# Scores from two fp32r parts in two 64-row array tiles, in place of three bf16 parts in the full array

## The chip, the cores and the metric

One NeuronCore of a Trainium2 chip runs the whole program; the other cores are idle. The metric is the device time of one launch in microseconds, all loads and stores included, as the median of several runs.

## The reference, cut to what matters

The program is one transformer layer with adaptive layer norm over 16 batches of 256 tokens, 256 features, 16 heads of 16 features. Attention is causal; the feed-forward part is two experts, one with gelu and one with relu, of which each token takes one. All arrays are float32.

```python
h = layernorm(x) * (1 + ca) + sa
q = h @ w_dq.T @ w_uq.T                      # 192 wide in between
k, v = split(h @ w_dkv.T @ w_ukv.T)          # 64 wide in between
attn = softmax(einsum('bhqd,bhkd->bhqk', q, k) * 0.25 + causal_mask)
x = x + ga * (einsum('bhqk,bhkd->bhqd', attn, v) @ w_out.T)
h = layernorm(x) * (1 + cb) + sb
x = x + gb * where(top_expert == 0, ffn_gelu(h), ffn_relu(h))
```

## The kernel before

Each batch is two tiles of 128 tokens. To keep float32's precision on a matrix engine that multiplies shorter numbers, an operand is split in a high part and a rest. The projections and the experts use two fp32r parts and three products each (`product`, L333 to L335). The scores use three bf16 parts of q and of k: `SPLITS` lists the six pairs of parts that are kept, and since a head has only 16 features, the six pairs are laid under one another in the partitions: 6 x 16 = 96 rows (`R`). So one matmul over 96 rows is the sum of the six products.

The layout is made by DMA. ACT writes part 0 from PSUM (`first_part`, L743), DVE the rest and part 1 (`part_rest` L984, `second_part` L990), POOL part 2 (`q_third` L1222, `k_third` L1228). Then SyncE's queue copies each part, [128, 512] bf16, to each 16-row band of `qs` or `ks` where it is wanted (`stack`, L282): 12 transfers of 128 KB a batch. `qs` and `ks` have two buffers, by parity of the batch; `stack` of batch n waits until all score chunks of batch n-2 that read the buffer are done (`wait(sp, st_done, CH * (b.n - 1))`).

Scores are computed twice for each batch, in six chunks of 1024 PSUM columns each time:
- `s_chunk` (L382) makes rows of queries in `ps_s`. ACT copies a chunk to SBUF (L794), POOL hides what lies past the diagonal (L1246), DVE takes the row maxima (`row_max`, L933).
- `split_maxima` (L941 to L948) splits the negated maxima in three bf16 parts, `turn_maxima` (L470) transposes them on PE, ACT copies them to `mx_rows` (L774), and a DMA (`load_maxima`, L271) puts them as three more rows under `qs`, against three rows of ones under `ks`.
- `st_chunk` (L401, and the mask as a matmul L405) makes the transposed scores less the maxima in `ps_t`, now over `RM` = 99 rows; ACT takes the exponentials (L806) into `p0` and `p1`. `values` (L419, L420) multiplies them with v, four heads at a time in four 32-column tiles of the array.

Everything runs as a software pipeline over batches. Each engine has its own `step`, a list of calls written out by hand, in which `at(k)` is the batch k steps behind. Per step PE runs: `turn_maxima(at(2))`, `turn_values(at(3))`, `up`, `expand_v`, `gate`, `turn_attn`, then `st_chunk(at(2), 0)`, then `up`, `project_out(at(3))`, and from `s_chunk(at(1), 0)` on the other score chunks, mixed with the down projections, to `st_chunk(at(2), 5)`, `values(at(2), 0)`, `s_chunk(at(1), 5)`, `values`, `expand_k(at(0))`, `up(at(3), 0)`, `up(at(3), 1)`. SyncE's step issues, in this order and all to one queue: `stack_q(at(1), 2)`, `stack_q(at(0), 0)`, `stack_q(at(0), 1)`, `stack_k(at(0), 0)`, `load_gates`, `prefetch_x`, `load_maxima(at(1))`, `stack_k(at(0), 1)`, `store`, `stack_k(at(0), 2)`. `load_maxima(at(1))` in it is for the maxima that PE turns in the next step.

Of the kernel before, what the change touches and what calls it, by code (L numbers as in the profile page):

```python
# [29 lines left out]
SPLITS = ((0, 0), (0, 1), (0, 2), (1, 0), (1, 1), (2, 0))  # L30
# [23 lines left out]
def block_kernel(nc, x, w_dq, w_uqT, w_dkvT, w_ukT, w_uvT, w_outT, wgT, waT, wbT, ba, bb, cT, wmod, out):  # L54
# [13 lines left out]
    RM = R + 3  # L68
# [3 lines left out]
    LOADS = 16 * NSPLIT  # L72
# [12 lines left out]
    with ctx:  # L85
# [27 lines left out]
        parts_q, parts_k = sb("parts_q", [P, 3, KT * S], BF16), sb("parts_k", [P, 3, KT * S], BF16)  # L113
        rest_q, rest_k = sb("rest_q", [P, KT * S]), sb("rest_k", [P, KT * S])
        ckv = sb("ckv", [P, S], F32R)
        v = [sb(f"v{i}", [P, TT, NH, HD + 1]) for i in range(2)]
        qs = [sb(f"qs{i}", [RM, NH, S], BF16) for i in range(2)]
        ks = [sb(f"ks{i}", [RM, NH, S], BF16) for i in range(2)]

        score_rows = [sb(f"score_rows{i}", [P, 1024]) for i in range(2)]  # L120
        mx = sb("mx", [P, TT, NH])
        mx_parts = sb("mx_parts", [P, TT, 3, NH], BF16)
        mx_rest = sb("mx_rest", [P, TT, NH])
        mx_rows = sb("mx_rows", [3 * NH, S], BF16)
# [36 lines left out]
        cT_raw, c_silu = mx[:], mx_rest[:]  # L161
# [14 lines left out]
        q_done, q1_ready, qr_ready, q2_ready, q3_ready, k_done, k1_ready, kr_ready, k2_ready, k3_ready = (sem(n) for n in  # L176
            "q_done q1_ready qr_ready q2_ready q3_ready k_done k1_ready kr_ready k2_ready k3_ready".split())
# [52 lines left out]
        def _(sp):  # L230
# [35 lines left out]
            def load_maxima(b):  # L266

                if b.off:
                    return
                sp.wait_ge(mt_ready, b.n + 1)  # L270
                sp.dma_start(qs[b.parity][R:RM, :, :], mx_rows[:]).then_inc(maxrows_in, 16)  # L271

            def stack(b, part, side, parts, stacks, ready, done):

                if b.off:
                    return
                wait(sp, st_done, CH * (b.n - 1))
                wait_alone(sp)
                sp.wait_ge(ready[part], b.n + 1)
                for n in range(NSPLIT):  # L280
                    if SPLITS[n][side] == part:
                        sp.dma_start(stacks[b.parity][n * HD:(n + 1) * HD, :, :], parts[:, part, :]).then_inc(done[b.parity], 16)  # L282

            def stack_q(b, part):
                stack(b, part, 0, parts_q, qs, (q1_ready, q2_ready, q3_ready), q_in)

            def stack_k(b, part):
                stack(b, part, 1, parts_k, ks, (k1_ready, k2_ready, k3_ready), k_in)
# [24 lines left out]
            def step(at):  # L313
                stack_q(at(1), 2)
# [8 lines left out]
                stack_k(at(0), 2)  # L323
# [6 lines left out]
        def _(pe):  # L330
            def product(outp, left, right, start, stop, **kw):
# [7 lines left out]
                "T1": ((h32_ready, 1, 1),), "Q": ((q1_ready, 1, 1), (qr_ready, 1, 1)), "CKV": ((ckv_ready, 1, 1),),  # L339
                "K": ((k1_ready, 1, 1), (kr_ready, 1, 1)), "V": ((v_ready, 1, 1),), "MT": ((mt_ready, 1, 1),),  # L340
# [25 lines left out]
            def s_chunk(b, c):  # L366
# [12 lines left out]
                tile, heads = (0, range(8 * c, 8 * c + 8)) if c < 2 else (1, range(4 * c - 8, 4 * c - 4))  # L379
                width = P * (tile + 1)  # L380
                for n, h in enumerate(heads):
                    mm = pe.matmul(ps_s[:, n * width:(n + 1) * width], qs[b.parity][0:R, h, tile * P:(tile + 1) * P],  # L382
                                   ks[b.parity][0:R, h, 0:width], start=True, stop=True)
                mm.then_inc(s_done, 1)

            def st_chunk(b, c):
# [6 lines left out]
                if c == 0:  # L393
                    pe.wait_ge(maxrows_in, 16 * (b.n + 1))
# [5 lines left out]
                for h in range(n):  # L400
                    pe.matmul(ps_t[:, h * width:(h + 1) * width], ks[b.parity][0:RM, h0 + h, tile * P:(tile + 1) * P],  # L401
                              qs[b.parity][0:RM, h0 + h, tile * P:S], start=h % a_bank == 0, stop=False)
# [59 lines left out]
            def turn_maxima(b, *users):  # L462
# [3 lines left out]
                pe.wait_ge(max_split, 4 * (b.n + 1))  # L466
                bank_left(users)
                wait_alone(pe)
                for t in range(TT):
                    mm = pe.transpose(mt_out[:, t * P:(t + 1) * P], mx_parts[:, t, :, :].rearrange("p c h -> p (c h)"), ident_b[:])  # L470
# [185 lines left out]
            mt_out = BANK["MT"][0:3 * NH, 0:P].bitcast(BF16)  # L656
# [3 lines left out]
        def _(act):  # L660
            act.wait_ge(mod_in, 32)
            act.activation(c_silu, cT_raw, ACT.Silu).then_inc(silu_ready, 1)
# [82 lines left out]
            def q_first(b):  # L745
                first_part(b, BANK["Q"], parts_q, q_done, qr_ready, q_in, q1_ready)

            def k_first(b):
                first_part(b, BANK["K"], parts_k, k_done, kr_ready, k_in, k1_ready)
# [18 lines left out]
            def maxima_rows(b):  # L768
# [4 lines left out]
                wait(act, maxrows_in, 16 * b.n)  # L773
                act.activation(mx_rows[:], BANK["MT"][0:3 * NH, 0:P].bitcast(BF16), ACT.Copy).then_inc(mt_ready, 1)  # L774
# [21 lines left out]
            def exponentials(b, c):  # L796
# [9 lines left out]
                act.activation((p0, p1)[tile][:, h0:h0 + n, :], ps_t[:].rearrange("p (h s) -> p h s", h=n), ACT.Exp, scale=SCALE).then_inc(exp_done, 1)  # L806
# [33 lines left out]
        def _(dve):  # L840
# [81 lines left out]
            def row_max(b, c):  # L922
# [3 lines left out]
                if c == 0:  # L926

                    wait(dve, max_split, 4 * b.n)
                if c < 2:
                    dst, n = mx[:, 0, 8 * c:8 * c + 8], 8  # L930
                else:
                    dst, n = mx[:, 1, 4 * c - 8:4 * c - 4], 4
                dve.tensor_reduce(dst, score_rows[c % 2][:].rearrange("p (h k) -> p h k", h=n), AX_X, ALU.max).then_inc(max_done, 1)  # L933

            def split_maxima(b):
# [5 lines left out]
                dve.tensor_scalar(mx_parts[:, :, 0, :], mx[:], -1.0, None, ALU.mult).then_inc(max_split, 1)  # L941
                dve.wait_ge(max_split, 4 * b.n + 1)
# [371 lines left out]
```

## Time and profile before

| | |
|---|---|
| median of 3 runs | 604.27 us (600.83 to 604.54) |
| the profiled execution | 601.1 us, its span 599.3 us |
| PE busy | 520.9 us, 87% of the span, 4912 matmuls |
| PE weight loads | 446.5 us |
| DVE busy | 480.9 us, 80% |
| ACT busy | 365.5 us, 61% |
| POOL busy | 309.7 us, 52% |
| DMA queue q1 | 43760 packets, 43.19 MB, 37.2% of the 16 engines' span |
| chain that ended last | PE 31%, DVE 29%, DMA 14%, issue 11%, POOL 6% |

Busy time of PE counts each matmul with the time its result needs to come out, so a busy PE is not one at its peak; how densely matmuls follow one another is read from their start times. The pipeline fills in the first 118 us, runs evenly from there to 507 us, and drains after. A line such as `306.02 0.38 PE L405 MATMUL ... x2` in the timeline is a run of two matmuls that starts at 306.02 us and lasts 0.38 us to the end of the last.

### The profile page before, as it was taken

How to read it: one execution, taken by the hardware profiler on the slowest of the kernel's cores; microseconds unless marked ns; L12 is line 12 of the kernel's file. 1: busy time of each engine (PE TensorE's matmuls, PEld its weight loads, DVE VectorE, ACT ScalarE, POOL GpSimd, SP SyncE). 2: the span in 40 equal slices, each digit the busy share in tenths (PEclk: the TensorE clock that was granted, in tenths of full speed). 3: DMA queues.
4: the chain of work that ended last, by engine and by line, in shares of the span. 5: the costliest groups of instructions: out<-in, count | busy, mean ns of one | idle time of the engine just before them, and what ended most of it. 6: DMA issues, size and time to landing. Idle time of an engine off the chain costs nothing.

```text
span 599.3 us, 14257 instructions
## 1 busy us (share of the span) xinstructions
PE 520.9 (87%) x4912; PEld 446.5 (75%) x4912; DVE 480.9 (80%) x949; ACT 365.5 (61%) x521; POOL 309.7 (52%) x300
## 2 busy tenths in 40 slices
PE   5435757999898989999999999999999999999874
PEld 4324545788787878787878888788979788888774
DVE  3548255779798989899898999899999899887572
ACT  2424644868575866667676858585766667675320
POOL 6334223455554665655656555556665655552441
PEclk9856696999999999999999999999999999999997
DMA  8835252433516080715244251708080715210100
GB/s 246 208 39 83 25 91 55 78 67 59 104 34 128 2 161 1 128 32 93 66 67 92 48 111 28 131 5 154 0 161 2 136 26 91 53 39 2 36 19 18
DMA packets 43802, 43.74 MB, mean 73 GB/s; under 512 B 5344, under 2 KB 40800, under 8 KB 43760
## 3 DMA queue, kind: packets, MB, share of 16 engines
q1 hardware_dynamic: 43760, 43.19, 37.2%
q8 instruction: 25, 0.41, 0.3%
q14 instruction: 17, 0.14, 0.1%
HBM read 13.39 MB, written 4.23 MB: 29 GB/s over the span
## 4 chain that ended last, share of the span: by engine, by line
PE 31%; DVE 29%; DMA 14%; issue 11%; POOL 6%; ACT 4%; SPq 3%; DVEq 1%; POOLq 0%; ACTq 0%
DVE mx L933 8%; DMA xs<-x 7%; DMA qs<-mx_rows 4%; PE ps_s L382 4%; PE ps_t L401 3%; DVE z L872 3%; SPq L282 2%; DMA qs<-parts_q 2%; POOL xs L1186 2%; PE ps_c L333 2%; PE ps_t L405 2%; DVE hid L1079 2%; PE ps_o L333 2%; ACT score_rows L794 2%; PE ps_c L335 2%
## 5 line engine op out<-in xcount | busy, mean ns | idle before, releaser
L794 ACT ACTIVATE score_rows<-ps_s 128x1024 f32<-128x1024 f32 x96 | 98.9, 1031 | 78.2 <-PE ps_s L382 59.8
L1246 POOL TENSOR_SCALAR_AFFINE_SELECT score_rows<-score_rows 128x512 f32<-128x512 f32 (+1 forms) x96 | 83.0, 865 | 101.8 <-ACT score_rows L794 101.8
L933 DVE TENSOR_REDUCE mx<-score_rows 128x4 f32<-128x1024 f32 (+1 forms) x96 | 114.0, 1210 | 4.4 <-POOL score_rows L1246 4.3
L806 ACT ACTIVATE p<-ps_t 128x1024 f32<-128x1024 f32 x96 | 98.4, 1025 | 16.9 <-PE ps_t L405 16.7
L382 PE MATMUL ps_s<-ks,qs 96*128 96x256 bf16 (+1 forms) x512 | 62.6, 259 | 19.6 <-DMA qs<-parts_q 15.9
L401 PE MATMUL ps_t<-qs,ks 99*128 99x256 bf16 (+1 forms) x512 | 60.7, 253 | 15.2 <-DMA qs<-mx_rows 14.3
L1186 POOL TENSOR_TENSOR xs<-z,xs 128x512 f32<-128x512 f32 (+1 forms) x16 | 30.7, 1922 | 61.7 <-DVE z L1022 61.7
L382 PEld LDWEIGHTS ps_s<-ks,qs 96*128 96x128 bf16 x512 | 36.8, 103 | 32.0 <-DMA qs<-parts_q 17.2
L401 PEld LDWEIGHTS ps_t<-qs,ks 99*128 99x128 bf16 x512 | 38.0, 100 | 23.1 <-DMA qs<-mx_rows 10.3
L856 DVE BATCH_NORM_STATS2 ln_st<-xs 128x6 f32<-128x256 f32 (+1 forms) x64 | 23.9, 415 | 35.2 <-DMA xs<-x 27.7
L1234 POOL TENSOR_TENSOR hid_lo<-hid,hid_hi 128x512 fp32r<-128x512 f32 x32 | 42.8, 1351 | 4.8 <-DVE hid_hi L1092 4.8
L405 PE MATMUL ps_t<-past_b,ident_b 128*128 128x256 bf16 (+1 forms) x192 | 45.2, 317 | 0.0
L1177 POOL TENSOR_TENSOR ln_rs<-ln_ve,neg_half 128x2 f32<-128x2 f32 x32 | 24.2, 755 | 35.9 <-DVE ln_ve L862 35.8
L333 PE MATMUL ps_o<-wb,hid_hi 128*128 128x256 f32 x128 | 39.5, 308 | 2.3 <-DVE hid_lo L1098 2.3
L419 PE MATMUL ps_o<-p,v 128*17 128x256 f32 x512 | 41.3, 384 | 0.2 <-ACT oT L688 0.2
L1092 DVE CAST hid_hi<-hid 128x512 fp32r<-128x512 f32 x64 | 36.1, 564 | 5.0 <-ACT hid L784 4.9
L333 PE MATMUL ps_a<-wb,hid_hi 128*128 128x256 f32 x128 | 39.8, 311 | 0.0
L333 PE MATMUL ps_c<-g_hi,wa 128*128 128x256 f32 x128 | 37.6, 294 | 1.6 <-issue 1.6
L334 PE MATMUL ps_o<-wb,hid_hi 128*128 128x256 f32 x128 | 36.7, 287 | 0.0
L335 PE MATMUL ps_o<-wb,hid_lo 128*128 128x256 f32 x128 | 36.6, 286 | 0.0
L334 PE MATMUL ps_c<-g_lo,wa 128*128 128x256 f32 x128 | 36.1, 282 | 0.0
L335 PE MATMUL ps_c<-g_hi,wa 128*128 128x256 f32 x128 | 36.1, 282 | 0.0
(166 smaller groups left out, 1648.1 us busy)
## 6 DMA issues: line engine op xcount, KB each, us to landing
qs<-parts_q SPq DMA_DIRECT2D x96, 128.0 KB, 3.9
ks<-parts_k SPq DMA_DIRECT2D x96, 128.0 KB, 4.4
xs<-x SPq DMA_DIRECT2D x16, 256.0 KB, 5.3
gates<-gates_scratch SPq DMA_DIRECT2D x16, 256.0 KB, 4.6
out<-xs SPq DMA_DIRECT2D x16, 256.0 KB, 3.5
p<-wmod SPq DMA_DIRECT2D x1, 1024.0 KB, 6.3
p<-waT SPq DMA_DIRECT2D x1, 1024.0 KB, 8.7
p<-wmod SPq DMA_DIRECT2D x1, 512.0 KB, 5.2
```

The source lines that it names most:

```text
L333: pe.matmul(outp, left[0], right[0], start=start, stop=False, **kw)
L334: pe.matmul(outp, left[0], right[1], start=False, stop=False, **kw)
L335: return pe.matmul(outp, left[1], right[0], start=False, stop=stop, **kw)
L382: mm = pe.matmul(ps_s[:, n * width:(n + 1) * width], qs[b.parity][0:R, h, tile * P:(tile + 1) * P], ks[b.parity][0:R, h, 0:width], start=T ...
L401: pe.matmul(ps_t[:, h * width:(h + 1) * width], ks[b.parity][0:RM, h0 + h, tile * P:(tile + 1) * P], qs[b.parity][0:RM, h0 + h, tile * P:S ...
L405: mm = pe.matmul(diag, ident_b[:], past_b[:].unsqueeze(1).to_broadcast([P, a_bank, P]), start=False, stop=True)
L794: act.activation(score_rows[c % 2][:], ps_s[:], ACT.Copy).then_inc(scores_out, 1)
L806: act.activation((p0, p1)[tile][:, h0:h0 + n, :], ps_t[:].rearrange("p (h s) -> p h s", h=n), ACT.Exp, scale=SCALE).then_inc(exp_done, 1)
L933: dve.tensor_reduce(dst, score_rows[c % 2][:].rearrange("p (h k) -> p h k", h=n), AX_X, ALU.max).then_inc(max_done, 1)
L1186: pool.tensor_tensor(rows, gated[:], rows, ALU.add).then_inc(x1_ready, 1)
L1234: pool.tensor_tensor(hid_lo[:, 2 * u:2 * u + 2, :], hid32[:, u, :, :], hid_hi[:, 2 * u:2 * u + 2, :].bitcast(F32), ALU.subtract).then_inc( ...
L1246: pool.affine_select(out=diag, in_=diag, compare_op=ALU.is_ge, fill=NEG, base=0, pattern=[[0, n], [-1, P]], channel_multiplier=1).then_inc ...
```

## The change

- q and k are split in two fp32r parts. `SPLITS` keeps three pairs, so a head needs 48 rows. The stack buffers are fp32r and have two halves of partitions: heads of even number in the pair from row 0, the others from row `ODD` = 64, eight columns blocks (`H2`) deep.
- Each `stack` call now copies a part to each band in two transfers, one for each half. A transfer is again 128 KB. Part 0 of q goes to two bands, part 1 to one; the same for k.
- `s_chunk` and `st_chunk` issue pairs of matmuls, rows 0 to 47 (49) and rows 64 to 111 (113), each writing a PSUM bank of its own. Column counts stay 128 and 256.
- The maxima are split in two fp32r parts by two DVE instructions in place of four, transposed as f32, and loaded by two transfers.
- DVE's `part_rest` and `second_part` become one instruction (`low_part`); POOL's `q_third` and `k_third` go. SyncE's calls for the third parts go too.
- The exponentials are written to `p0` and `p1` in the order of the pairs; `ks` is filled with ones as a whole at the start.

```diff
-SPLITS = ((0, 0), (0, 1), (0, 2), (1, 0), (1, 1), (2, 0))
+SPLITS = ((0, 0), (0, 1), (1, 0))
+ODD = 64
...
-    RM = R + 3
+    RM = R + 2
+    H2 = NH // 2
...
-        qs = [sb(f"qs{i}", [RM, NH, S], BF16) for i in range(2)]
+        qs = [sb(f"qs{i}", [ODD + RM, H2, S], F32R) for i in range(2)]
...
-                sp.dma_start(qs[b.parity][R:RM, :, :], mx_rows[:]).then_inc(maxrows_in, 16)
+                for k in range(2):
+                    sp.dma_start(qs[b.parity][ODD * k + R:ODD * k + RM, :, :].bitcast(F32), mx_rows[NH * k:NH * (k + 1), :].bitcast(F32)).then_inc(maxrows_in, 16)
...
                 for n in range(NSPLIT):
                     if SPLITS[n][side] == part:
-                        sp.dma_start(stacks[b.parity][n * HD:(n + 1) * HD, :, :], parts[:, part, :]).then_inc(done[b.parity], 16)
+                        for k in range(KT):
+                            row = ODD * k + n * HD
+                            sp.dma_start(stacks[b.parity][row:row + HD, :, :].bitcast(F32), parts[:, part, k * S:(k + 1) * S].bitcast(F32)).then_inc(done[b.parity], 16)
...
             def step(at):
-                stack_q(at(1), 2)
                 stack_q(at(0), 0)
                 stack_q(at(0), 1)
                 stack_k(at(0), 0)
...
                 stack_k(at(0), 1)
                 store(at(4))
-                stack_k(at(0), 2)
...
-                for n, h in enumerate(heads):
-                    mm = pe.matmul(ps_s[:, n * width:(n + 1) * width], qs[b.parity][0:R, h, tile * P:(tile + 1) * P],
-                                   ks[b.parity][0:R, h, 0:width], start=True, stop=True)
+                for n, h in enumerate(pairs):
+                    for k in range(2):
+                        rows = slice(ODD * k, ODD * k + R)
+                        mm = pe.matmul(ps_s[:, k * 512 + n * width:k * 512 + (n + 1) * width], qs[b.parity][rows, h, tile * P:(tile + 1) * P],
+                                       ks[b.parity][rows, h, 0:width], start=True, stop=True)
...
-                for h in range(n):
-                    pe.matmul(ps_t[:, h * width:(h + 1) * width], ks[b.parity][0:RM, h0 + h, tile * P:(tile + 1) * P],
-                              qs[b.parity][0:RM, h0 + h, tile * P:S], start=h % a_bank == 0, stop=False)
+                for h in range(a_bank):
+                    for k in range(2):
+                        rows = slice(ODD * k, ODD * k + RM)
+                        pe.matmul(ps_t[:, k * 512 + h * width:k * 512 + (h + 1) * width], ks[b.parity][rows, h0 // 2 + h, tile * P:(tile + 1) * P],
+                                  qs[b.parity][rows, h0 // 2 + h, tile * P:S], start=h == 0, stop=False)
...
-                dve.tensor_scalar(mx_parts[:, :, 0, :], mx[:], -1.0, None, ALU.mult).then_inc(max_split, 1)
-                dve.wait_ge(max_split, 4 * b.n + 1)
-                dve.scalar_tensor_tensor(out=mx_rest[:], in0=mx[:], scalar=-1.0, in1=mx_parts[:, :, 0, :],
+                dve.tensor_scalar(mx_parts[:, :, :, 0, :], mx[:], -1.0, None, ALU.mult).then_inc(max_split, 1)
+                dve.wait_ge(max_split, 2 * b.n + 1)
+                dve.scalar_tensor_tensor(out=mx_parts[:, :, :, 1, :], in0=mx[:], scalar=-1.0, in1=mx_parts[:, :, :, 0, :].bitcast(F32),
                                          op0=ALU.mult, op1=ALU.subtract).then_inc(max_split, 1)
-                dve.wait_ge(max_split, 4 * b.n + 2)
-                dve.tensor_copy(mx_parts[:, :, 1, :], mx_rest[:]).then_inc(max_split, 1)
-                dve.wait_ge(max_split, 4 * b.n + 3)
-                dve.tensor_tensor(mx_parts[:, :, 2, :], mx_rest[:], mx_parts[:, :, 1, :], ALU.subtract).then_inc(max_split, 1)
...
-                dve.tensor_tensor(rest[:], src[:], parts[:, 0, :], ALU.subtract).then_inc(rest_ready, 1)
...
-                dve.tensor_copy(parts[:, 1, :], rest[:]).then_inc(ready, 1)
...
+                dve.tensor_tensor(parts[:, 1, :], src[:], parts[:, 0, :].bitcast(F32), ALU.subtract).then_inc(ready, 1)
...
-                q_second(at(1))
...
-                k_rest(at(1))
+                k_low(at(1))
                 hidden_high(at(4), 0)
-                k_second(at(1))
...
-                q_rest(at(0))
+                q_low(at(0))
...
-                q_third(at(0))
-                k_third(at(0))
                 hidden_low(at(3), 0)
```

## Rows read from the trace of the kernel before

**Rows 1.** Windows: length; busy per engine; clock, DMA share, GB/s; the even part.

```profile
118.00:507.00 389.00, 371.12 (x3654) 321.33 (x3653) 355.50 (x695) 269.37 (x385) 226.55 (x216) 1.00 0.40 74
```

**Rows 2.** The transposes of the maxima between 118 and 507 us, by line.

```profile
L470 PE MATMUL ps_c<-ident_b,mx_parts x26: 216/217/236, 118.1 to 506.6; 128*48 128x128 bf16 x26
```

**Rows 3.** Waits of PE from 204 to 492 us: in total, times, longest.

```profile
PE ps_c L470 <- DVE mx_parts L948: 5.8, 9, 0.7
PE ps_t L401 <- DMA qs<-mx_rows: 2.0, 6, 0.5
PE ps_c L333 <- DVE a_lo L1009: 1.7, 2, 1.2
```

**Rows 4.** Timeline of PE, one step: start, length, line, count, idle before.

```profile
306.02 0.38 PE L405 MATMUL ps_t<-past_b,ident_b 128*128 128x256 bf16 x2
...
314.33 0.27 PE L470 MATMUL ps_c<-ident_b,mx_parts 128*48 128x128 bf16 x2 [0.65 <-DVE mx_parts L948]
...
318.08 0.60 PE L437 MATMUL ps_b<-ident,attn 128*128 128x128 f32 x4
318.98 0.62 PE L401 MATMUL ps_t<-qs,ks 99*128 99x128 bf16 x8 [0.31 <-DMA qs<-mx_rows]
...
338.20 0.38 PE L405 MATMUL ps_t<-past_b,ident_b 128*128 128x256 bf16 x2
```

**Rows 5.** Timeline of SyncE's queue in the same step: issues of DMAs.

```profile
306.55 3.67 SPq L282 DMA_DIRECT2D qs<-parts_q  x5
310.32 1.83 SPq L282 DMA_DIRECT2D ks<-parts_k  x3
312.64 0.37 SPq L263 DMA_DIRECT2D gates<-gates_scratch  x1
313.32 0.40 SPq L239 DMA_DIRECT2D xs<-x  x1
315.13 0.79 SPq L271 DMA_DIRECT2D qs<-mx_rows  x1
316.02 1.23 SPq L282 DMA_DIRECT2D ks<-parts_k  x2
```

**Rows 6.** Windows, while the eight transfers ahead of the maxima are served.

```profile
307.76:314.83 7.07, 6.42 (x81) 5.11 (x82) 6.87 (x11) 4.78 (x8) 4.45 (x5) 1.00 0.98 145
```

**Rows 7.** Timeline of DVE and of POOL around the split of the maxima.

```profile
311.29 1.20 DVE L941 TENSOR_SCALAR mx_parts<-mx 128x32 bf16<-128x32 f32 x1
312.52 1.11 DVE L943 SCALAR_TENSOR_TENSOR mx_rest<-mx,mx_parts 128x32 f32<-128x32 f32 x1
...
311.17 1.28 POOL L1204 TENSOR_TENSOR xs<-y,xs 128x512 f32 x1 [0.15 <-POOL y L1194]
312.41 1.18 POOL L1222 TENSOR_TENSOR parts_q<-rest_q,parts_q 128x512 bf16<-128x512 f32 x1
```

**Rows 8.** Timeline of PE: score chunks, and `values` between two projections.

```profile
294.18 0.62 PE L382 MATMUL ps_s<-ks,qs 96*128 96x128 bf16 x8
...
296.72 0.61 PE L382 MATMUL ps_s<-ks,qs 96*128 96x256 bf16 x4
...
310.34 0.28 PE L335 MATMUL ps_c<-g_hi,wa 128*128 128x256 f32 x1
310.55 0.65 PE L419 MATMUL ps_o<-p,v 128*17 128x256 f32 x8
...
311.21 0.64 PE L419 MATMUL ps_o<-p,v 128*17 128x256 f32 x8
311.64 0.43 PE L420 MATMUL ps_o<-p,v 128*17 128x128 f32 x8
312.00 0.39 PE L333 MATMUL ps_a<-g_hi,wa 128*128 128x256 f32 x1
312.22 0.28 PE L334 MATMUL ps_a<-g_lo,wa 128*128 128x256 f32 x1
```

**Rows 9.** Windows near the end: columns as in rows 1.

```profile
581.80:585.20 3.40, 1.54 (x14) 1.35 (x13) 3.37 (x8) 0.00 (x0) 0.72 (x1) 1.00 0.00 0
585.20:588.60 3.40, 3.40 (x19) 3.40 (x18) 0.66 (x4) 0.00 (x0) 0.00 (x0) 0.51 0.00 0
```

## What the change does to the time: the prediction

> **What bounds the kernel now.** I read the page first, then the windows, PE's waits, and last the timelines of one step. The windows show that from 118 to 507 us PE is busy 95% of the time at its full clock, DVE 91%, ACT and POOL far less [rows 1]. The maxima of 13 batches are turned in that stretch, the first at 118.1 and the last at 506.6 us, so a step is 388.5 / 12 = 32.4 us [rows 2]. PE paces it: its waits there sum to about 1 us a step, most of them for the split maxima and for the DMA of the maxima [rows 3].
>
> The step's shape matters more than the sum. I cut it where SyncE is let go. The last mask matmul of chunk 5 ends at 306.40 us; `st_chunk` 0 of the next batch starts at 318.98; chunk 5 of that batch ends at 338.58 [rows 4]. Leg A is thus 12.58 us, leg B 19.60 us. Leg B is matmuls nearly back to back. In leg A two chains run side by side. One is PE's own: 12.58 less the waits of 0.65 and 0.31 us is 11.6 us of work. The other is the queue: the first stack transfer is issued at 306.55, 0.15 us after chunk 5 frees the buffer; then come 5 of q, 3 of k, the gates, x, and only then the maxima, issued at 315.13 [rows 5]; PE starts 3.85 us later. The eight stack transfers (8 x 131 KB) are served in 7.07 us at 145 GB/s with the DMA engines' share at 0.98 [rows 6], so 0.88 us each, a full queue that serves in order. So two things in leg A are nearly level now, and the queue is the later one, by 0.31 us.
>
> **The change, part by part: the queue.** A batch has 12 stack transfers of 128 KB before and after, so the bytes don't change; their order does. Before, 3 + 2 of q and 3 of k stand ahead of the maxima and 4 come later. After, part 0 of q is 2 bands x 2 halves = 4, part 1 is 2, part 0 of k is 4: 10 stand ahead and 2 come later. Two more at 0.88 us is 1.8 us, in a queue that is already full. The start can't move forward, since `stack` still waits for chunk 5. Issuing isn't the limit: ten at 0.61 to 0.73 us [rows 5] end by 313.1 us, gates and x by 314.3. The second transfer of maxima costs SyncE another 0.8 us, which lies inside the longer backlog. Leg A becomes 12.58 + 1.8 = 14.4 us. Bounds: 0 if the transfers were served as fast as other 128 KB pieces and the queue emptied in time, 2.6 us if the second maxima transfer also counts in full. x also stands ahead of the maxima and lands 1.8 us later, for DVE's statistics, but PE's `st_chunk` 0 is later by as much, so DVE's later work keeps its distance from PE's.
>
> **DVE and POOL.** Two casts to bf16 go, two of the four splits of maxima, two POOL subtractions. L941 and L943 take 1.20 and 1.11 us for 32 numbers a partition, and each ends within 0.05 us of a POOL operation beside it: L1204 at 312.45, L1222 at 313.59 [rows 7]. L1222 goes, so L943's successor should be short and the maxima ready some 1.3 us earlier. That removes PE's wait of 0.65 us at L470. It is worth nothing in leg A, because the DMA of the maxima then waits in the queue; if the queue weren't there, it would give 0.65 us. The other savings lie on engines with slack once the step is longer. ACT's instructions keep their sizes. I cost all these at nothing; the cover is the queue's 14.4 us.
>
> **PE.** Spacing first, from start times at the full clock. In bf16, eight matmuls of 128 columns run in 0.62 us and four of 256 in 0.61 us; less about 0.22 and 0.28 us for the last one, that is 0.056 and 0.109 us apiece [rows 8]. Score matmuls cost per batch 32 x 0.109 + 32 x 0.056 = 5.3 us. fp32r products of 256 columns follow at 0.12 us (312.22 less the 0.10 us below). No row has fp32r at 128 columns. The nearest are the f32 transposes, four in 0.60 us, 0.11 apiece with a 128 x 128 f32 weight load [rows 4], and bf16's 0.056. I take 0.107, because the load of f32 weights shows itself to be that long: the first product after `values` lasts 0.39 in place of 0.28 us [rows 8].
>
> Do two tiles overlap? `values` puts four heads in four column tiles: 16 records, eight of 256 and eight of 128 columns, from 310.55 to 311.21, 0.66 us [rows 8]. At bf16's spacing they would take 1.3 us one after another, and they are f32, so they do overlap. I assume that row tiles do too, loads included: a pair costs what one matmul did, 0.118 or 0.107 us. Four chunks of four 128-column pairs: 3 x 0.107 + 0.053 = 0.37 each; eight chunks of two 256-column pairs: 0.118 + 0.107 = 0.225 each; 3.3 us in all, 2.0 less than now.
>
> Entering and leaving cost. L335 to L419 is 0.21 us where 0.12 is normal; after the last L420 the next product starts 0.09 us late and is 0.10 us longer [rows 8]. So a switch is 0.09 us, and 0.10 more when an f32 load follows that can't be hidden. Nine times a batch PE enters the row tiles (s and st chunks that are neighbours share one): 9 x 0.19 = 1.7 us. Six exits go to the bf16 mask, 0.11 each, and two to f32 work, 0.19 each; the one to `values` is paid already: 1.1 us. The sum is 3.3 + 2.8 - 5.3 = +0.8 us a batch. About 0.3 of it disappears in waits that PE has anyway in leg B (a_lo, 1.7 us in 9 steps [rows 3]) and before `st_chunk` 0. I take +0.5 us for leg B. Bounds: -2.0 if switches are free; if the tiles don't overlap, 32 x 0.118 + 32 x 0.107 + 2.8 - 5.3 = +4.7.
>
> On the switch the Trainium skill speaks against the change: "TensorEngine Tiling (Array Packing)", Key Properties, says that changing the tiling mode, not only the tile, drains the engine. The extra 0.09 us at L419 agrees; the sum is the one above. The same page's table of theoretical speedup gives up to 2x for contractions of 64 rows or fewer; by that alone leg B would be shorter by 2.0 us, which is the second rival.
>
> **The sum.** (14.4 - 12.58) + 0.5 = +2.3 us a step. It holds in the 14 steps in which stacks are loaded beside the maxima of an earlier batch: 32 us. Filling and draining: batches 0, 1 and 15 pay the tiles, about +2 us, and the first stacks lose a stage of splitting, about -2 us. Against the profiled execution's own 601.1 us (span 599.3) that is 633 us; that execution lies 3 us under the median of three, 604.27, so I say 635.
>
> **The rivals.**
> 1. The queue and the switches, as above: 635, its own range 622 to 650. 40%.
> 2. Tiles overlap and switching is free: leg B 17.6, leg A 14.4, the step 32.0: 604 - 14 x 0.2 = about 601. For it: `values` overlaps so well. Against: L335 to L419. 16%.
> 3. The tiles, or their weight loads, take turns. Leg B +3.7 to +4.7: 604 + 14 x (1.8 + 4.0) = 685. For it: no row shows row tiles. 13%.
> 4. On the other side: the queue gives no delay. It decides if ten transfers and x are served before about 317 us in the step shown, for example because f32 halves go faster than 0.88 us each. Then leg A falls to PE's 11.6 us and DVE's relief counts: -1.0 + 0.5 = -0.5 us a step, 597. For it: the queue is late by only 0.31 us now. Against: share 0.98 in that stretch. 13%.
> 5. The clock. PE's idle time before `st_chunk` 0 grows from two pieces of 0.65 and 0.31 us to one of about 2.8 us. Near the end of the trace a stretch with PE busy 1.54 of 3.40 us is followed by one at the lower level of 1.2 GHz, 0.51 of the full clock, for 3.4 us [rows 9]. If each step paid that once, it would cost up to 1.7 us: 635 + 14 x 1.7 = 659. Against: the rest of the step is dense. 15%.
> 6. Rivals 2 and 4 together: -2.5 us a step, 569. 3%.
>
> **How the numbers follow.** The range leaves out case 6, about half of case 3 and a few per cent at the edges of the others: 594 to 680. A measurement of this kernel can tell about 1% from no change. Faster by more: case 6, half of 4 and a little of 2: 0.12. Within 1%: the rest of 2 and of 4: 0.20. Slower: cases 1, 3 and 5: 0.68.
>
> **What would show it.** In the profile after: `st_chunk` 0 starts about 14.4 us after the last mask matmul of the batch before, and PE's wait in front of it, for the DMA of maxima, is the longest, 2 us or more, while the wait for `mx_parts` is gone. The chunks: first matmul of a chunk about 0.2 us later than now after the product ahead, pairs starting together, 0.107 to 0.12 us from pair to pair. Leg B about 20.1 us. The granted clock stays 1.00 from 118 us on. Wrong are: pairs at 0.2 us or more (case 3), no late starts (case 2), ten stack transfers served in 7 us (case 4), a clock under 1.00 (case 5).

## The result: 680 us, and the profile after

The changed kernel takes 680.17 us (median of 4 runs, 679.92 to 680.96) against 602.55 us for the kernel before on the same chip. The ratio is 1.130 with a 95% interval of 1.125 to 1.134. The forecast was 635 us, 32 us of loss, with a range up to 680. The direction and the place of the loss came out as forecast; the loss is 78 us, more than twice as large, and the time lies just outside the range.

First the profiled execution by windows: length; busy per engine; clock, DMA share, GB/s. The stretch is the even part, as in [rows 1] for the kernel before.

```profile
118.00:560.00 442.00, 389.74 (x3572) 332.14 (x3570) 312.29 (x628) 263.56 (x375) 189.24 (x184) 0.91 0.40 65
```

PE is busy 88% of the time in place of 95%, and its clock is 0.91 in place of 1.00. So both idle time and slow time were added. The waits of PE from 204 to 560 us (total, times, longest), then DVE's and SyncE's in the same view:

```profile
PE ps_t L410 <- DMA qs<-mx_rows: 43.1, 10, 4.5
PE ps_c L446 <- DVE z L882: 0.5, 1, 0.5
...
DVE ln_st L866 <- DMA xs<-x: 48.1, 10, 5.8
...
SPq L52 <- PE ps_t L414: 234.2, 9, 26.6
```

One wait is left: 4.3 us in every step, for the DMA of the maxima. In [rows 3] it was 2.0 us in all. Here is one step of PE's timeline; [rows 4] answers to it.

```profile
346.29 0.39 PE L414 MATMUL ps_t<-past_b,ident_b 128*128 128x256 bf16 x2
...
353.65 0.38 PE L479 MATMUL ps_c<-ident,mx_parts 128*32 128x128 f32 x2
...
357.27 0.60 PE L446 MATMUL ps_b<-ident,attn 128*128 128x128 f32 x4
362.26 1.11 PE L410 MATMUL ps_t<-qs,ks 50*128 50x128 f32 x8 [4.39 <-DMA qs<-mx_rows]
363.30 1.04 PE L414 MATMUL ps_t<-past_b,ident_b 128*128 128x512 bf16 x2
...
383.84 0.39 PE L414 MATMUL ps_t<-past_b,ident_b 128*128 128x256 bf16 x2
```

PE has finished its own work of leg A at 357.87 us and then stands. When it starts again, eight matmuls that need 0.66 us at the full clock take 1.11. The windows of the same step show why; the clock is the column before the last two.

```profile
350.00:357.10 7.10, 7.10 (x82) 6.28 (x81) 4.16 (x10) 3.94 (x9) 5.06 (x5) 1.00 1.12 130
357.30:362.20 4.90, 0.57 (x6) 0.33 (x3) 1.10 (x5) 0.76 (x2) 0.00 (x0) 0.84 1.04 212
362.20:365.60 3.40, 3.34 (x17) 2.87 (x18) 1.89 (x5) 1.16 (x1) 0.71 (x1) 0.50 0.03 11
365.60:369.20 3.60, 3.60 (x29) 3.47 (x29) 2.17 (x6) 1.15 (x2) 0.00 (x0) 0.74 0.00 0
369.20:384.00 14.80, 14.80 (x132) 12.69 (x128) 14.53 (x27) 12.01 (x17) 9.48 (x9) 1.00 0.00 0
```

The DMA engines are full (share 1.04 to 1.12) until the maxima are in, and idle after. The clock falls to 0.50 in the idle time and stays there for 6.8 us, over the first score chunks and projections of leg B. SyncE's queue in this step, beside [rows 5]:

```profile
346.84 3.77 SPq L286 DMA_DIRECT2D qs<-parts_q  x6
350.71 2.47 SPq L286 DMA_DIRECT2D ks<-parts_k  x4
353.39 0.43 SPq L264 DMA_DIRECT2D gates<-gates_scratch  x1
354.13 0.40 SPq L240 DMA_DIRECT2D xs<-x  x1
354.57 1.40 SPq L273 DMA_DIRECT2D qs<-mx_rows  x2
356.07 1.24 SPq L286 DMA_DIRECT2D ks<-parts_k  x2
```

Of the kernels below I give the two legs, read from the profiled execution. To compare them I measure from start to start: leg A from the start of the last mask matmul of chunk 5 to the start of `st_chunk` 0, leg B from there to the next last mask matmul, each a mean over ten steps of the even part. "Clock low" is how long the clock stands at 0.50 in one of these steps. Each ratio is against the kernel before, run on the same chip (medians 602.55 to 604.03 us). Medians and ratios leave out launches in a slower state of the chip, but the profiled executions of act_queue (689.95 us) and spread_full (664.13 us) were such launches, so their legs count for less.

| kernel | median us | ratio, 95% interval | leg A | leg B | step | clock low |
|---|---|---|---|---|---|---|
| before | 602.55 | 1 | 12.83 | 19.53 | 32.36 | never |
| after | 680.17 | 1.130, 1.125 to 1.134 | 15.80 | 21.77 | 37.57 | 6.8 us, each |
| act_queue | 680.99 | 1.133, 1.125 to 1.140 | 16.33 | 21.56 | 37.89 | 3.4 or 6.8 us, each |
| before_ten | 626.61 | 1.039, 1.035 to 1.043 | 14.83 | 19.24 | 34.07 | never |
| two_maxima | 606.78 | 1.003, 0.999 to 1.008 | 13.37 | 19.25 | 32.61 | never |
| ten_two | 641.17 | 1.060, 1.054 to 1.067 | 15.09 | 19.76 | 34.85 | 3.4 us, some |
| fill32 | 654.98 | 1.088, 1.083 to 1.094 | 15.67 | 19.74 | 35.41 | never |
| eight_ahead | 632.41 | 1.051, 1.046 to 1.056 | 13.70 | 20.81 | 34.51 | 3.4 us, most (6.8 us, one) |
| spread | 646.27 | 1.073, 1.065 to 1.081 | 11.39 | 24.20 | 35.59 | 3.4 to 10 us |
| spread_full | 656.18 | 1.088, 1.077 to 1.098 | 11.49 | 25.05 | 36.54 | 3.4 or 6.8 us, most |
| spread_before | 667.65 | 1.108, 1.100 to 1.116 | 11.90 | 25.55 | 37.45 | 6.8 us, each |
| balanced | 608.97 | 1.012, 1.005 to 1.018 | 12.48 | 19.78 | 32.26 | never |
| balanced_full | 614.69 | 1.024, 1.017 to 1.030 | 12.36 | 20.73 | 33.09 | never |
| before_gates | 602.95 | 1.000, 0.995 to 1.004 | 12.11 | 20.29 | 32.40 | never |

The last mask matmul of batch 0 starts at 76.8 us before and at 83.3 us after; that of batch 14 at 527.4 and at 606.3. So the fill (the stretch up to the first of these two marks) lost 6.6 us, the 14 steps 72.3 us (5.16 each), the drain 0.2: together the 79.0 us between the spans of 599.3 and 678.3.

### The profile page after: what moved, and what is told of

Read it like the earlier page. It is cut to its first block, busy times and chain, and to the rows that moved or that the text cites. A ratio compares the mean times of both kernels' runs of the same rounds, so it can differ in the third digit from the quotient of the medians.

```text
span 678.3 us, 14114 instructions
## 1 busy us (share of the span) xinstructions
PE 560.5 (83%) x4912; PEld 472.4 (70%) x4912; DVE 440.7 (65%) x885; ACT 367.0 (54%) x521; POOL 267.7 (39%) x268
## 4 chain that ended last, share of the span: by engine, by line
PE 58%; DMA 17%; SPq 14%; issue 5%; DVE 4%; ACT 2%; POOL 0%; POOLq 0%; DVEq 0%; ACTq 0%
DMA qs<-mx_rows 14%; SPq L286 11%; PE ps_t L410 7%; PE ps_t L414 6%; PE ps_s L389 6%; PE ps_o L338 4%; PE ps_c L338 4%; PE ps_o L339 4%; PE ps_o L340 4%; PE ps_c L339 3%; PE ps_c L340 3%; PE ps_a L338 3%; PE ps_a L340 3%; PE ps_a L339 2%; PE ps_o L428 2%
## 5 line engine op out<-in xcount | busy, mean ns | idle before, releaser
L410 PE MATMUL ps_t<-qs,ks 50*128 50x256 f32 (+1 forms) x512 | 60.2, 342 | 73.0 <-DMA qs<-mx_rows 72.3
L410 PEld LDWEIGHTS ps_t<-qs,ks 50*128 50x128 f32 x512 | 44.6, 229 | 82.5 <-DMA qs<-mx_rows 49.4
L389 PE MATMUL ps_s<-ks,qs 48*128 48x256 f32 (+1 forms) x512 | 58.4, 331 | 16.4 <-DMA ks<-parts_k 14.0
L1177 POOL TENSOR_TENSOR xs<-z,xs 128x512 f32<-128x512 f32 (+1 forms) x16 | 27.7, 1733 | 104.3 <-DVE z L1015 104.3
L389 PEld LDWEIGHTS ps_s<-ks,qs 48*128 48x128 f32 x512 | 39.8, 205 | 34.8 <-issue 21.4
L414 PE MATMUL ps_t<-past_b,ident_b 128*128 128x256 bf16 (+1 forms) x192 | 53.1, 364 | 0.0
L1072 DVE TENSOR_SCALAR hid<-ps_o,bias_a 128x256 f32<-128x256 f32 x32 | 14.0, 479 | 38.5 <-PE ps_o L340 38.5
L1085 DVE CAST hid_hi<-hid 128x512 fp32r<-128x512 f32 x64 | 29.3, 457 | 14.4 <-ACT hid L793 13.5
L338 PE MATMUL ps_c<-g_hi,wa 128*128 128x256 f32 x128 | 37.3, 291 | 1.6 <-issue 1.6
L1091 DVE TENSOR_TENSOR hid_lo<-hid,hid_hi 128x512 fp32r<-128x512 f32 x32 | 37.5, 1212 | 0.0
L340 PE MATMUL ps_o<-wb,hid_lo 128*128 128x256 f32 x128 | 36.5, 285 | 0.0
```

The costliest lines, as they stand in the source:

```text
L338: pe.matmul(outp, left[0], right[0], start=start, stop=False, **kw)
L340: return pe.matmul(outp, left[1], right[0], start=False, stop=stop, **kw)
L389: mm = pe.matmul(ps_s[:, k * 512 + n * width:k * 512 + (n + 1) * width], qs[b.parity][rows, h, tile * P:(tile + 1) * P], ks[b.parity][rows ...
L410: pe.matmul(ps_t[:, k * 512 + h * width:k * 512 + (h + 1) * width], ks[b.parity][rows, h0 // 2 + h, tile * P:(tile + 1) * P], qs[b.parity] ...
L414: mm = pe.matmul(diag, ident_b[:], past_b[:].unsqueeze(1).to_broadcast([P, a_bank, P]), start=False, stop=True)
```

## The experiments

**Is it the queue's order, and does another queue help?** The theory was that the maxima stand behind ten stack transfers in SyncE's queue, so they should go past them in a queue of their own.

```diff
 def load_maxima(b):   # taken out of SyncE's step, put behind ACT's copy to mx_rows
-    sp.dma_start(qs[b.parity][ODD * k + R:...], mx_rows[...])
+    act.dma_start(qs[b.parity][ODD * k + R:...], mx_rows[...])
```

> The changed kernel, with the two transfers of maxima issued from ACT's queue right after ACT has written mx_rows, so that they don't stand behind the stack transfers of SyncE's queue. Theory Q (queue and clock): the 4.4 us wait before st_chunk 0 goes, leg A falls from 15.9 to PE's own work of about 11.7 us, the clock stays at its upper level, leg B falls from 21.7 to about 19.4 us; step 31.1 to 31.7 us, time about 595 us. Theory T (the row tiles themselves cost): leg B stays near 21.7 us, step 33.4 us, time about 622 us.

680.99 us: no gain; both theories had forecast one. The timeline of ACT's queue, DVE and PE in one step:

```profile
399.13 1.28 ACTq L778 DMA_DIRECT2D qs<-mx_rows  x2
...
405.44 0.75 DVE L861 BATCH_NORM_STATS2 ln_st<-xs 128x6 f32 x2 [2.98 <-DMA xs<-x]
...
407.32 0.93 PE L401 MATMUL ps_t<-qs,ks 50*128 50x128 f32 x8 [4.08 <-DMA qs<-mx_rows]
```

The transfers are issued 8.2 us before PE may start. In the trace their first packet is served only at 404.05 us, 4.9 us after the issue, and the last at 406.27. In the last batch, where no stack transfers stand ahead, the first packet comes 1.6 us after the issue. So the backlog of SyncE's queue holds up ACT's as well; a queue of one's own doesn't pass it. What has to change is how much has been issued before.

**Does the order alone delay the bf16 kernel?** One line of its SyncE step moves, so that ten transfers stand ahead there too.

```diff
-                load_maxima(at(1))
                 stack_k(at(0), 1)
+                load_maxima(at(1))
```

> The kernel before, bf16 and full array, with one edit: the two transfers of part 1 of k stand ahead of the maxima in SyncE's order, ten stack transfers in place of eight. Theory Q: leg A grows from 12.6 to about 14.6 us, PE waits about 3 us before st_chunk 0; about 630 us if the clock holds, up to 665 us if it falls in each step. Theory T: the queue matters little without the tiles, under 612 us.

626.61 us, leg A +2.00 us. PE's wait in one step:

```profile
267.90 0.62 PE L401 MATMUL ps_t<-qs,ks 99*128 99x128 bf16 x8 [2.41 <-DMA qs<-mx_rows]
```

The clock stays at 1.00 from 134 us on, in spite of 2.1 to 2.4 us of idle time in every step. The order is worth 2.0 us of leg A, in bf16 and in the full array. Leg B gives 0.3 us back (19.24 against 19.53), so the step is 1.7 us longer.

**What does the second transfer of the maxima cost?** The kernel before, with its maxima loaded twice (the second time to rows that nothing reads).

```diff
-                sp.dma_start(qs[b.parity][R:RM, :, :], mx_rows[:]).then_inc(maxrows_in, 16)
+                for k in range(2):
+                    sp.dma_start(qs[b.parity][R + 3 * k:RM + 3 * k, :, :], mx_rows[:]).then_inc(maxrows_in, 16)
```

> The kernel before with the transfer of the maxima issued twice, the second copy to three spare rows, and st_chunk 0 waiting for both. If the second transfer as such is what costs about 1 us of leg A in the changed kernel (its issue, and a second pass through the same two or three DMA engines), leg A grows from 12.8 to about 13.7 us and the time to about 616 us. If it is the longer pieces of 1 KB, nothing changes: 603 us.

606.78 us, ratio 0.999 to 1.008: no difference in the total that can be told from none, but leg A is 0.54 us longer and PE's wait is larger than in [rows 3]:

```profile
PE ps_t L402 <- DMA qs<-mx_rows: 6.8, 9, 0.8
```

The landing times in the traces say where it goes. Counted from the start of the last mask matmuls of one step (306.02 us before, 346.29 after):

| lands after, us | before | after |
|---|---|---|
| 8th stack transfer | 10.58 | 10.81 |
| 10th stack transfer | (later) | 12.65 |
| x | 12.53 | 14.43 |
| maxima, complete | 12.84 | 15.85 |

x is 1.9 us later; the maxima come 0.31 us after x before and 1.42 us after. So 1.1 us belong to the maxima themselves. Each of the two transfers brings eight 1 KB pieces to each of two rows. In the trace of act_queue, where nothing else is in their queue, these pieces are served two at a time; the 48 pieces of 512 bytes of the kernel before are served three at a time. In two_maxima the gap between x and the maxima is 1.37 us in the step I read, so the second transfer by itself makes nearly the whole gap; but x lands earlier there, and leg A grows by no more than the 0.54 us.

**Both together, in bf16.** This was run last: the two edits above in the kernel before.

> The bf16 kernel before, with both changes of the queue at once and no other: all ten transfers of parts stand ahead of the maxima, and the maxima are loaded in two transfers (the second writes three rows that no matmul reads). Leg A is the time from the last mask matmul of a batch to st_chunk 0 of the next, 12.83 us in the kernel before. Alone, the order gave +2.0 and the second transfer +0.54. Theory: the queue side explains the loss without the tiles or fp32r. Leg A 15.4 to 15.8 us (the changed kernel has 15.80), PE idle ahead of st_chunk 0 about 3 us or more, and the clock falls in the steps: with that, 14 x (2.8 + 1.7) over 602.5, about 665 us; should the clock stay at 1.00, 14 x 2.7 over, about 640. Rival, that the fp32r kernel loses by what PE does in its chunks: leg A at most 15.4, no clock fall, under 640. If leg A comes out at 15.4, the remaining 0.4 us of the changed kernel belong to the shape of its maxima transfers (2 rows of 1 KB pieces); if at 15.8, to the order and the count alone.

641.17 us. Leg A is 15.09 us, 0.3 below what was expected and 0.7 below the changed kernel's: the two queue effects give 2.3 of its 3.0 us. The second transfer adds 0.3 us to before_ten. At two steps PE's timeline reads

```profile
201.56 0.62 PE L402 MATMUL ps_t<-qs,ks 99*128 99x128 bf16 x8 [2.56 <-DMA qs<-mx_rows]
...
304.77 0.62 PE L402 MATMUL ps_t<-qs,ks 99*128 99x128 bf16 x8 [2.50 <-DMA qs<-mx_rows]
```

and the windows behind these two starts, with the clock before the last two columns:

```profile
201.56:206.00 4.44, 4.26 (x40) 3.90 (x41) 4.30 (x14) 2.31 (x2) 0.71 (x1) 1.00 0.13 34
...
304.77:309.50 4.73, 4.72 (x30) 4.58 (x31) 1.98 (x6) 1.02 (x1) 0.00 (x0) 0.64 0.13 29
```

After 2.56 us of waiting the clock stayed, after 2.50 it fell, 1.3 us into the work. So neither theory holds whole: the clock falls in bf16 too, but in less than half of the steps and for 3.4 us. The queue by itself reproduces 37 of the 78 us. The last 0.7 us of leg A isn't settled (the shape of the fp32r maxima's transfers is one candidate, and no run tried it by itself); in the step I read, the changed kernel had its eighth stack transfer 0.25 us later than ten_two, and its maxima came 1.4 us after the last transfer ahead of them, against 1.1.

**What is the clock worth?** 32 matmuls of which nothing is used fill PE's idle time in the changed kernel; they write a PSUM tile that `st_chunk` 0 overwrites.

```diff
+                wait(pe, exp_done, CH * b.n + c)
                 if c == 0:
+                    for n in range(32):
+                        pe.matmul(ps_t[:, (n % 4) * 256:(n % 4 + 1) * 256], wa[0][:, 0, 0:P], wa[0][:, 1, 0:256], start=True, stop=True)
                     pe.wait_ge(maxrows_in, 32 * (b.n + 1))
-                wait(pe, exp_done, CH * b.n + c)
```

> The changed kernel, with 32 more matmuls of 256 columns (about 3.7 us, their result is overwritten) before the wait for the maxima in st_chunk 0, so that PE doesn't idle there. Leg A is unchanged in both theories, 15.9 us. Theory Q: the clock stays at its upper level in every step, leg B falls from 21.7 to 19.2 to 19.6 us, step 35.3 us, time about 646 us. Theory T: leg B stays near 21.7 us whatever the clock, time 680 us.

654.98 us, 25 us under the changed kernel. PE's timeline in one step, and the even part:

```profile
345.67 4.07 PE L403 MATMUL ps_t<-wa 128*128 128x256 f32 x32
...
350.21 0.66 PE L412 MATMUL ps_t<-qs,ks 50*128 50x128 f32 x8 [0.47 <-DMA qs<-mx_rows]
...
118.00:540.00 422.00, 415.33 (x4015) 359.55 (x4014) 308.02 (x641) 269.08 (x383) 197.13 (x189) 1.00 0.42 68
```

Leg A stays (15.67), leg B falls from 21.77 to 19.74. So the clock costs 2.0 us a step. What is left of leg B is the tiles' cost: 0.2 us over the kernel before, or 0.5 us over before_ten (19.24), a bf16 kernel that also waits in leg A.

**Eight ahead again, in the changed kernel.** The second band of part 0 of k goes behind the maxima.

```diff
-                stack_k(at(0), 0)
+                stack_k(at(0), 0, (0,))
                 load_gates(at(2))
                 prefetch_x(at(-1))
                 load_maxima(at(1))
+                stack_k(at(0), 0, (2,))
```

> The changed kernel, with two of the four transfers of part 0 of k moved behind the maxima in SyncE's order: eight stack transfers ahead of them, as in the kernel before. Theory Q: leg A falls by 2.0 us to 13.9 us and PE's wait to about 2.4 us. If a wait of that length leaves the clock up, leg B is 19.4 us and the time about 618 us; if not, 652 us. Theory T: leg B stays at 21.7 us with the clock up, 652 us.

632.41 us, leg A 13.70: 2.1 us back for two transfers. Compared with the 12.83 us of the kernel before, 0.87 us are left for the maxima. The time lies between the forecasts for a clock that stays (618) and one that falls in every step (652). PE's waits:

```profile
PE ps_t L411 <- DMA qs<-mx_rows: 20.9, 9, 2.9
```

Each wait is 2.0 to 2.9 us, and in seven of the ten steps the clock still falls: leg B is 19.7 us where it doesn't and 20.9 to 22.4 where it does. The shortest and the longest wait show that the length doesn't decide it; below are PE's timeline and the windows behind these two starts:

```profile
197.11 1.10 PE L411 MATMUL ps_t<-qs,ks 50*128 50x128 f32 x8 [2.00 <-DMA qs<-mx_rows]
...
232.80 0.66 PE L411 MATMUL ps_t<-qs,ks 50*128 50x128 f32 x8 [2.90 <-DMA qs<-mx_rows]
```

```profile
197.11:201.11 4.00, 4.00 (x22) 3.52 (x23) 3.00 (x9) 1.82 (x2) 0.71 (x1) 0.57 0.45 99
232.80:236.80 4.00, 4.00 (x36) 3.65 (x36) 3.52 (x11) 1.03 (x1) 0.71 (x1) 1.00 0.30 75
```

Set beside before_ten this leaves a question. There the waits are 2.1 to 2.4 us and the clock falls in none of the ten steps; here nearly all waits are 2.0 to 2.3 us and it falls in seven. So the fp32r tiles may make the clock fall sooner, besides the wait. No run separates the two.

**x and the maxima ahead of all k.** To empty the queue for them, k and the gates were put last; the same edit was made to the kernel before.

```diff
-                stack_k(at(0), 0)
-                load_gates(at(2))
                 prefetch_x(at(-1))
                 load_maxima(at(1))
+                stack_k(at(0), 0)
                 stack_k(at(0), 1)
                 store(at(4))
+                load_gates(at(2))
```

> The changed kernel with SyncE's order changed alone: q's transfers, x, the maxima, then all six of k, the store, and the gates last. Six stack transfers and x stand ahead of the maxima, none of the gates. Theory D (what costs is the backlog of the DMA engines ahead of the maxima, and the fall of the clock that the wait brings): leg A falls from 15.8 to PE's own 11.7 us, the clock stays up, leg B is 19.7 us; step 31.4 us, with up to 1 us more if k's transfers are late for s_chunk 0; time 592 to 606 us. Theory T (the tiles cost): leg B above 21 us with the clock up, 620 us.

> The kernel before with the same order: q, x, the maxima, then k, the store, the rest of k, the gates. Five stack transfers and x ahead of the maxima. Theory D: PE's wait of 0.3 us for the maxima goes, the wait of 0.65 us for their split stays, since DVE makes it; leg A 12.4 us, leg B 19.5 us, time about 598 us, 1% under the kernel before. Theory T: the same, no difference.

646.27 and 667.65 us; both forecasts missed. Leg A fell even below the forecasts of 11.7 and 12.4, to 11.39 and 11.90, without a wait for the maxima. But SyncE has to wait until the maxima are ready, and all of k is behind it. Waits of PE and SyncE in spread, and of PE in spread_before:

```profile
PE ps_s L389 <- DMA ks<-parts_k: 17.1, 7, 2.5
...
SPq L273 <- ACT mx_rows L783: 27.4, 9, 3.2
```

```profile
PE ps_s L382 <- DMA qs<-parts_q: 42.7, 10, 4.4
```

The wait moved from `st_chunk` 0 to the first `s_chunk`, and the clock falls there. In spread this chunk waits for the new k; in spread_before for the third part of q, which SyncE issues right behind the last of k. In spread SyncE's 3.0 us a step are time in which the DMA engines could have moved k.

**Tiles or full array, in that order.** In spread_full each matmul of a pair uses the whole array, as many matmuls as before, one after another. Each then sums two heads, so this kernel doesn't compute the attention; it serves to time the array alone.

```diff
-                        rows = slice(ODD * k, ODD * k + R)
+                        rows = slice(0, ODD + R)
```

> As spread, but the score matmuls run over all rows 0 to 111 (113) of the full array, one after another, so that each is the sum of two heads and the output isn't the reference's; counts and columns are the same. It takes the row tiles away and keeps fp32r. Theory O (tiles overlap and cost their switches): 64 matmuls in turn at 0.107 to 0.118 us are 7.2 us a batch against 3.3 + 2.8, so leg B grows by about 1.0 us against spread: 15 us more in all. If tiles were no better than turns, spread_full would be 40 us faster by the switches.

656.18 us against 646.27 of spread; leg B 25.05 against 24.20. The direction is the forecast one, but the clock falls for 3.4 to 10 us in steps of both, at different places, so this pair doesn't give the price of the array. balanced_full, below, does.

**A middle order.** eight_ahead, with the gates also behind the maxima.

```diff
-                load_gates(at(2))
                 prefetch_x(at(-1))
                 load_maxima(at(1))
                 stack_k(at(0), 0, (2,))
                 stack_k(at(0), 1)
+                load_gates(at(2))
```

> The changed kernel with SyncE's order: q's six transfers, two of part 0 of k, x, the maxima, the other two of part 0 of k, part 1 of k, the gates, the store. Eight stack transfers and x ahead of the maxima as in eight_ahead, but not the gates. Theory D: leg A 11.9 us, k's transfers land at about the time of s_chunk 0, so neither wait is longer than 1 us; the clock stays up, leg B 19.7 to 20.2 us; step 31.6 to 32.1 us, time 592 to 602 us, as fast as the kernel before or 1% faster. If the tiles or the clock cost without a wait, leg B is above 20.5 us, time over 610 us.

608.97 us: 71 us less than the changed kernel, by the order of SyncE's calls alone. Waits of PE and the even part by windows:

```profile
PE ps_t L411 <- DMA qs<-mx_rows: 9.4, 9, 1.2
...
118.00:510.00 392.00, 375.53 (x3695) 317.29 (x3693) 316.51 (x650) 272.66 (x387) 196.28 (x190) 1.00 0.44 74
```

The wait is 1.0 us a step, the clock stays up, and the step is 32.26 us, the same as before (32.36). The forecast of 592 to 602 us was missed: leg A is 12.48, not 11.9. The kernel is still 1.2% slower than the one before in total (0.5 to 1.8%), and that lies in the fill, below.

The same move of the gates in the kernel before:

> The kernel before with one edit in SyncE's order: the gates go behind the maxima and part 1 of k. Theory D: the maxima are no longer the later chain; PE's wait of about 0.65 us for the split of the maxima stays; leg A 12.4 us, leg B 19.5 us: 598 us. If the gates then come late for DVE, leg B grows and the time is 605 us or more.

602.95 us, ratio 0.995 to 1.004. Leg A gains 0.7, leg B loses as much: PE waits 11.6 us in 8 steps for q at the first `s_chunk`. The kernel before had nothing to win by this move.

And balanced with the full array, the edit of spread_full:

> As balanced, but the score matmuls run over rows 0 to 111 (113) of the full array, one after another, each the sum of two heads, so that the output isn't the reference's; counts and columns are the same. Theory O (pairs overlap, switches cost 0.1 to 0.2 us each): leg B grows by about 1.0 us, 15 us more than balanced. Theory T (tiles bring nothing but switches): leg B falls, up to 40 us less than balanced.

614.69 us. Leg B is 0.95 us longer than in balanced, so for fp32r parts two tiles save about 1 us a step over using the array whole. In the total it is only 6 us, not 13. The difference lies in the fill and the first steps after it, where balanced has the clock low for longer. (A part of the fill belongs to no kernel: the first score matmul starts between 35 and 41 us in the 14 traces, in both forms; in this pair at 40.5 in balanced and 35.3 in balanced_full.) Windows from 70 to 85 us, of the kernel before, of balanced, and of balanced_full:

```profile
70.00:85.00 15.00, 12.45 (x139) 8.84 (x138) 11.26 (x19) 10.72 (x15) 7.03 (x8) 1.00 0.47 68
```

```profile
70.00:85.00 15.00, 14.68 (x78) 10.63 (x76) 5.64 (x6) 10.07 (x13) 5.28 (x6) 0.50 0.01 2
```

```profile
70.00:85.00 15.00, 13.49 (x138) 10.18 (x137) 10.12 (x14) 11.38 (x15) 4.83 (x6) 1.00 0.37 57
```

In balanced PE shows as busy for 14.68 of 15 us and yet stays at the lower level. In this stretch it has mostly score chunks and projections to do. A matmul lasts longer at the lower level, so the busy times don't compare the work: it is 78 matmuls against 138.

## Why the prediction was right, and where it failed

**The queue, right.** "Two more at 0.88 us is 1.8 us": measured 2.0 (before_ten), 2.1 (eight_ahead), and 1.9 us in the landing time of x. The wait in front of `st_chunk` 0 is the longest, and the wait for `mx_parts` is gone. Rival 4, no delay, is excluded.

**DVE's relief, right.** The two splits of the maxima are short now, as the timelines of DVE and POOL show beside [rows 7]:

```profile
351.09 0.18 DVE L951 TENSOR_SCALAR mx_parts<-mx 128x32 fp32r<-128x32 f32 x1
351.30 0.19 DVE L953 SCALAR_TENSOR_TENSOR mx_parts<-mx,mx_parts 128x32 fp32r<-128x32 f32 x1
...
351.34 1.30 POOL L1195 TENSOR_TENSOR xs<-y,xs 128x512 f32 x1
```

That is 2.31 us down to 0.37. The forecast had only the second split short, by POOL's subtraction that is gone. The first is short too: it now comes before POOL's addition to xs (L1195), while in the kernel before it ran beside it (L1204). All this bought nothing: what PE turned earlier waited longer for its DMA.

**The tiles, right.** PE's timeline in leg B: a row chunk, an `st_chunk` and its mask, and then an `st_chunk` of four matmuls with the product ahead of it:

```profile
368.56 0.66 PE L389 MATMUL ps_s<-ks,qs 48*128 48x128 f32 x8
369.06 0.45 PE L410 MATMUL ps_t<-qs,ks 50*128 50x256 f32 x4
369.44 0.39 PE L414 MATMUL ps_t<-past_b,ident_b 128*128 128x256 bf16 x2
...
378.97 0.28 PE L340 MATMUL ps_b<-h_hi,wdkv 128*128 128x256 f32 x1
379.18 0.50 PE L410 MATMUL ps_t<-qs,ks 50*128 50x256 f32 x4
379.61 0.39 PE L414 MATMUL ps_t<-past_b,ident_b 128*128 128x256 bf16 x2
```

The second `st_chunk` enters 0.21 us after L340 in place of 0.12, and the mask follows 0.43 us later. The forecast's terms (0.19 for entering, 0.225 for two pairs, 0.11 for leaving) and the 0.12 of the product come to 0.645, and 378.97 to 379.61 is 0.64. The two matmuls of a pair start 4 ns apart. So pairs overlap and switches cost what `values` had shown; at the full clock leg B is 0.2 us longer than in the kernel before (fill32, balanced) and 0.5 longer than in before_ten, with 0.5 forecast. Rivals 2 and 3 are excluded. "TensorEngine Tiling (Array Packing)" of the Trainium skill, Key Properties, says that a change of mode drains the engine; the 0.09 us at each entry agrees with it.

**The maxima, wrong.** "The second transfer of maxima costs SyncE another 0.8 us, which lies inside the longer backlog." I counted only the issue. The transfer itself is also served at the end of the backlog, with nothing behind which it could hide, since PE waits for exactly it. The gap from x to the maxima became 1.1 us longer and leg A 0.9 to 1.0; the forecast had 0, with 0.8 as its bound. In bf16 a second transfer adds only 0.3 to 0.5 us to leg A (ten_two, two_maxima), so the count of transfers explains up to half; the rest stays open.

**The clock, wrong.** This was the large error. The forecast put the fall of the clock at nothing in its sum and made it a rival at 15% that comes in place of case 1. It is no separate case: it comes with PE's wait, which case 1 itself makes longer. At waits of 2.0 to 2.9 us, like the 2.8 that I forecast, it fell in four of ten steps (ten_two), in seven (eight_ahead) or in none (before_ten); at 4.2 to 4.5 us (after) it fell in every step, for 6.8 us. Its price of "up to 1.7 us" was for 3.4 us; measured 2.0 for 6.8 us, 28 us over 14 steps.

**The fill, wrong.** I had +2 and -2 us; it lost 6.6 us, 5.8 of them in the stretch in which the clock is low for longer (last section).

The sum again, with measured terms: queue 2.0, maxima 1.0, clock 2.0, tiles 0.2, that is 5.2 us a step. The terms are differences of the same legs, and the term of the maxima is what is left of leg A, so the sum has to close. 14 steps of 5.16 and 6.8 us at the ends are the 79 us between the two profiled executions.

## What to carry to other kernels

Where a result is awaited behind a full stretch of DMA, count bytes in the order of issue, on all queues together, and count the awaited transfer itself. A stall of the matrix engine is priced in two parts, the idle time and the slower clock after it, and these aren't alternatives. And try the order of the issues before judging an edit of the arithmetic: here it decided 71 of 78 us, while the arithmetic brought no gain in any order that was tried.

## What the hardware showed that was not expected

- A transfer on ACT's queue, issued at 399.13 us, was first served at 404.05, held up by SyncE's backlog; a second queue didn't give a second service.
- The clock stayed at 1.00 after PE waits of 2.1 to 2.4 us in before_ten, of 2.56 us in ten_two and of 2.90 us in eight_ahead; it fell after 2.50 us in ten_two and after 2.00 us in eight_ahead. Between 2.0 and 2.9 us it doesn't hang on the length of one wait alone.
- During the fill the clock stands at 0.50 from about 53 to 59 us on. It comes back after 27 to 31 us in the five kernels with row tiles and no filler (after, act_queue, eight_ahead, spread, balanced), and after 14 to 17 us in the six bf16 kernels and in the two that use the whole array with fp32r. From 70 to 85 us balanced_full had the full clock where balanced, with the same list of matmuls in tiles, had half. From the first score matmul to the last mask matmul of batch 0 it takes 40.8 us before, 42.7 in balanced_full, 45.3 in balanced and 46.5 after. That the tiles are the cause is what these runs suggest; balanced and balanced_full come nearest to a test, one trace each. It is where balanced lost most of its 1% (4.5 us) and where 5.8 of the 6.6 us of the changed kernel's fill went.
